# Layer 3's cross attention begun inside layer 2's read-back of expert rows, with stack rows 3 partitions apart

## The reference

```python
x = x + L2_xattn(layernorm(x), ctx, ...)     # 16 heads of 16 features
x = x + L2_ffn(layernorm(x), ...)            # 8 experts, 2 chosen per token, one shared expert
x = x + L3_xattn(layernorm(x), ctx, ...)
x = x + L3_ffn(layernorm(x), ...)

Q, K, V = heads(h @ Wq), heads(ctx @ Wk), heads(ctx @ Wv)
scores = einsum('bhnd,bhmd->bhnm', Q, K) * SCALE
out = softmax(scores) @ V                    # per head, then heads side by side
return out @ Wo + bo
```

## Time and profile before

| | us |
|---|---|
| median of 3 runs | 2535.56 (2533.76 to 2538.5) |
| the profiled execution's own time | 2525.97 |
| its span, first to last instruction | 2524.3 |
| TensorE busy | 2225.2 (88%) |
| VectorE busy | 1240.3 (49%) |
| ScalarE busy | 1044.0 (41%) |
| GpSimd busy | 535.8 (21%) |

### The profile page before, as it was taken

The page is one execution under the profiler, slowest core; times in us unless marked ns, Lnnn a source line. Parts: engine busy times, 40 slices in busy tenths (PEclk is TensorE's granted clock), DMA queues, the critical chain, the costliest instruction groups (busy, mean ns, idle before and its releaser), DMA issues. The chain is left out here.

```text
span 2524.3 us, 42831 instructions
## 1 busy us (share of the span) xinstructions
PE 2225.2 (88%) x13610; PEld 1643.9 (65%) x13611; DVE 1240.3 (49%) x2762; ACT 1044.0 (41%) x2555; POOL 535.8 (21%) x556
## 2 busy tenths in 40 slices
PE   8998399569998999898898998999997499989998
PEld 5664298444565874466785664679997256568887
DVE  4664300369876329876434664100000456577764
ACT  1564133214565523466532663124443036654332
POOL 1000200310122430121551000220001410054443
PEclk9999699789999999999998999999999699999999
DMA  7771143110000000000008741123221386110001
GB/s 190 154 173 70 46 169 109 46 42 0 26 0 15 26 17 0 25 0 3 13 6 143 133 79 74 36 106 121 73 106 47 99 154 129 36 34 20 26 25 34
DMA packets 110836, 164.29 MB, mean 65 GB/s; under 512 B 15273, under 2 KB 95257, under 8 KB 105721
## 3 DMA queue, kind: packets, MB, share of 16 engines
q1 hardware_dynamic: 101712, 140.68, 22.1%
q0 software_dynamic: 7680, 20.98, 2.6%
q10 hardware_dynamic: 1320, 1.03, 0.2%
HBM read 114.96 MB, written 47.32 MB: 64 GB/s over the span
## 5 line engine op out<-in xcount | busy, mean ns | idle before, releaser
L1043 DVE TENSOR_REDUCE xa_mx<-ps 128x2 f32<-128x512 f32 x384 | 247.0, 686 | 100.6 <-PE ps L695 99.5
L141 PE MATMUL ps<-ones 128*128 128x384 f32 (+1 forms) x450 | 164.7, 495 | 98.6 <-DMA ex_rows<-rows_out,rows_back 37.7
L902 ACT ACTIVATE xn_tok<-ps 128x512 f32<-128x512 f32 x384 | 210.6, 602 | 52.6 <-PE ps L703 50.4
L1482 PEld LDWEIGHTS ps<-ex_xT,ex_w 128*128 128x128 f32 x1792 | 210.5, 193 | 7.2 <-issue 4.4
L1482 PE MATMUL ps<-ex_xT,ex_w 128*128 128x128 f32 x1792 | 211.1, 276 | 3.8 <-issue 3.8
L1489 PE MATMUL ps<-ex_w,ex_h 128*128 128x256 f32 x896 | 202.7, 379 | 0.0
L141 PEld LDWEIGHTS ps<-ones 128*128 128x128 f32 x450 | 91.0, 223 | 142.9 <-issue 49.9
L695 PE MATMUL ps<-xa_ks,xa_qs 48*128 48x256 f32 (+1 forms) x768 | 157.7, 323 | 27.7 <-DMA xa_qs<-x_queries 9.1
L2147 PE MATMUL ps<-lo_w,lp_hs 128*128 128x512 f32 x384 | 176.1, 610 | 4.5 <-ACT lp_hs L2194 2.8
L1489 PEld LDWEIGHTS ps<-ex_w,ex_h 128*128 128x128 f32 x896 | 165.9, 190 | 20.2
L695 PEld LDWEIGHTS ps<-xa_ks,xa_qs 48*128 48x128 f32 (+1 forms) x768 | 106.6, 192 | 102.0 <-DVE xa_mx L1043 52.2
(11 more groups left out here) (343 smaller groups left out, 4815.8 us busy)
## 6 DMA issues: line engine op xcount, KB each, us to landing
xa_ks<-x_keys SPq DMA_DIRECT2D x144, 128.0 KB
xa_qs<-x_queries SPq DMA_DIRECT2D x144, 128.0 KB, 4.6
ex_w<-in_L0f_w_dram SPq DMA_DIRECT2D x16, 1024.0 KB, 7.0
ex_w<-in_L2f_w_dram SPq DMA_DIRECT2D x16, 1024.0 KB, 6.8
x_keys<-xa_khl SPq DMA_DIRECT2D x24, 512.0 KB, 5.6
x_queries<-xa_qhl SPq DMA_DIRECT2D x24, 512.0 KB, 3.0
ex_stage<-rows_in POOLq DMA_DIRECT2D x64, 128.0 KB, 2.3
rows_out<-ex_rows SPq DMA_DIRECT2D x56, 128.0 KB, 1.7
```

The source lines that it names most:

```text
L141: self.nc.tensor.matmul(self.ps[:, bank, 0:wide * P], self.ones[:], self.ones[:].unsqueeze(1).to_broadcast([P, wide, P]), start=True, stop ...
L902: nc.scalar.activation(pT[:, h % SLOTS].rearrange("p k q -> p (k q)"), c.ps[:, S_BANK + (HEADS * b + n) % 3], ACT.Exp).then_inc(exped.sem, 1)
L1043: nc.vector.tensor_reduce(mx[:, half, :, col], c.ps[:, M_BANK + h % 2].rearrange("p (t n) -> p t n", t=2), AX_X, ALU.max).then_inc(max_put ...
L1482: ins = nc.tensor.matmul(c.ps[:, f % 4, 0:P], w1[:, buf, k, f * P:(f + 1) * P], xT[:, k], start=(k == 0), stop=(k == KD - 1))
```

## The change

First, the parts of `xattn_phase` that were functions inside its engine blocks are now functions of the phase, which take the engine as an argument. With `room` given, `xattn_phase` is a generator that hands these functions out before it opens its own phase, and `expert_phases` calls them in its read-back. This is done for layer 2's experts with layer 3's attention:

```diff
+def experts_with_attention(c):
+    with ExitStack() as ctx:
+        room = c.sb("room", [P, tile_count(2), D], ctx=ctx)[:]
+        attention = xattn_phase(c, "L3x_", biased=True, room=room)
+        expert_phases(c, "L2f_", room, next(attention))
+        run(attention)
...
 (SyncE, behind the zeros)
+            if ahead:
+                sp.wait_ge(*out_stored(16 * tiles))
+                nxt.fetch_weights(sp)
+                for b in range(3):
+                    nxt.send_keys(sp, b)
+                    nxt.stack_keys(sp, b)
+                for b in range(2):
+                    nxt.send_queries(sp, b)
+                    nxt.stack_queries(sp, b)
...
 (TensorE)
-            pe.wait_ge(*back[2](16 * top * QUART))
+            if ahead:
+                pe.wait_ge(*nxt.weights_in(16))
+                for b in range(3):
+                    nxt.project_keys(pe, b)
+                    c.keep_busy(2, 0)
+                for b in range(2):
+                    nxt.turn_rows(pe, b)
+                    c.keep_busy(2, 0)
+                    pe.wait_ge(*nxt.scaled(1))
+                    nxt.project_queries(pe, b)
+                    c.keep_busy(2, 0)
+            pe.wait_ge(*back[2 + ahead](16 * top * QUART))
             c.keep_busy(8, 0)
...
 (ScalarE)
+            if ahead:
+                nxt.set_rows(act)
+                for b in range(3):
+                    nxt.lead_keys(act, b)
+                for b in range(2):
+                    nxt.put_rows(act, b)
+                    nxt.lead_queries(act, b)
...
 (VectorE, ahead of the additions, and in their loop)
+            if ahead:
+                nxt.scale_queries(dve)
+                for b in range(3):
+                    nxt.rest_keys(dve, b)
...
-                tile_stats(c, t)
+                ins = tile_stats(c, t)
+                if ahead and t == 3:
+                    nxt.find_moments(dve, 0, ins)
+                    for b in range(2):
+                        nxt.normalise_rows(dve, b)
+                elif ahead and t % 4 == 3 and t < 12:
+                    nxt.rest_queries(dve, t // 8)
...
 (GpSimd, in the loop of the gathers)
+            if ahead:
+                nxt.set_consts()
             for t in range(NT):
...
+                if ahead and t == 7:
+                    nxt.find_rstd(pool, 0)
```

Third, the form of the stacks, in all three attentions. The columns of Wq, Wk and the biases are reordered on their way in (`by_row`), so that in DRAM a row holds one feature of a head, and under it the eight pairs follow each other:

```diff
-                parts = dram["x_keys"][b].rearrange("(a g j r) t -> a j r g t", a=2, g=PAIRS, j=2)
+            parts = dram["x_keys"][b].rearrange("(a j r g) t -> a j r g t", a=2, g=PAIRS, j=2)
                 for j in range(2):
                     for n, part in enumerate((0, 0, 1)):
-                        at = 64 * j + HD * n
-                        sp.dma_start(ks[at:at + HD, b % K_BUFS].bitcast(F32), parts[part, j]
+                    at = 64 * j + n
+                    sp.dma_start(ks[at:at + 3 * HD - 2:3, b % K_BUFS].bitcast(F32), parts[part, j]
```

More of the change, by code:

```diff
@@ L493, in xattn_phase @@
     K_LOADS = 6 + 2 * masked
+    ahead = room is not None
     with ctx:
@@ new lines, in turn_rows @@
+        def turn_rows(pe, b):
+            if masked and b == 0:
+                pe.wait_ge(*ident_in(16))
+            pe.wait_ge(*normed(b + 1))
+            if ahead and b < 2:
+                pe.wait_ge(*k_rest(3))
+                pe.wait_ge(*q_rest(b))
+            elif b < 3:
+                pe.wait_ge(*k_rest(b + 1))
+                pe.wait_ge(*v_put(b - 1))
+            else:
+                pe.wait_ge(*v_put(b - 1))
+            for k in range(KD):
+                for t in range(2):
+                    ins = nc.tensor.transpose(c.ps[:, W_BANK, k * S + t * P:k * S + (t + 1) * P],
+                                              xs[:, 2 * (b % 2) + t, k * P:(k + 1) * P], c.ident[:])
+            ins.then_inc(turned.sem, 1)
@@ new lines, in project_keys @@
+        def project_keys(pe, b):
+            if ahead and b < 3:
+                pe.wait_ge(*k_rest(b))
+            else:
+                pe.wait_ge(*q_rest(b))
+            if b == 2 and not ahead:
+                pe.wait_ge(*v_put(1))
+                if masked:
+                    pe.wait_ge(*ctx_in[1](16))
+            for ch in range(KD):
+                for k in range(KD):
+                    ins = nc.tensor.matmul(c.ps[:, W_BANK, ch * S:(ch + 1) * S], wk[:, k, ch * P:(ch + 1) * P],
+                                           c.ctxT[:, k, b * S:(b + 1) * S], start=(k == 0), stop=(k == KD - 1))
+            ins.then_inc(k_proj.sem, 1)
@@ new lines, in project_queries, with put_rows @@
+        def project_queries(pe, b):
+            pe.wait_ge(*x_put(b + 1))
+            for ch in range(KD):
+                for k in range(KD):
+                    ins = nc.tensor.matmul(c.ps[:, W_BANK, ch * S:(ch + 1) * S], wq[:, k, ch * P:(ch + 1) * P],
+                                           c.xT[:, k, b * S:(b + 1) * S], start=(k == 0), stop=(k == KD - 1))
+            ins.then_inc(q_proj.sem, 1)
+        def put_rows(act, b):
+            act.wait_ge(*turned(b + 1))
+            nc.scalar.copy(c.xT[:, :, b * S:(b + 1) * S], bank).then_inc(x_put.sem, 1)
@@ new lines, in find_moments @@
+        def find_moments(dve, n, measured=None):
+            lo, hi = GROUPS[n]
+            if masked:
+                dve.wait_ge(*x_in[n](16))
+                for t in range(lo, hi):
+                    measured = tile_stats(c, t)
+            if measured:
+                chain.link(dve, measured)
+            st, at = c.stats[:, lo:hi], (slice(None), slice(lo, hi))
+            chain.link(dve, moments.join(dve, chain, at, (st[:, :, 0, 1], st[:, :, 1, 1]),
+                                         (st[:, :, 0, 2], st[:, :, 1, 2]), D // 4, mean[at], moments.total[at]))
+            nc.vector.tensor_scalar(var[at], moments.total[at], 1.0 / D, EPS, ALU.mult, ALU.add
+                                    ).then_inc(variance.sem, 1)
+            count[0] = chain.n
@@ L571, in _ @@
+        @block.sync
+        def _(sp):
+            if not ahead:
+                fetch_weights(sp)
             if masked:
@@ L1080, in _ @@
                 if h == 11:
[L1081 to L1083 removed]
+                    normalise_rows(dve, 2)
+                elif h == 13 and not ahead:
+                    rest_keys(dve, 2)
             for b in range(B):
```

540 lines of the change are left out of this document (269 added, 271 removed).

## The result

The changed kernel takes 2498.84 us in the median of 4 runs (2496.46 to 2507.45); the kernel before, beside it, 2534.66 us. The ratio is 0.987, with a 95% interval of 0.9851 to 0.989: 33 us faster, 28 to 38.

| us | before | after | gain | predicted |
|---|---|---|---|---|
| layer 0: to its last addition | 229.60 | 225.05 | 4.6 | 8.9 |
| layer 2: start to last addition | 213.58 | 207.21 | 6.4 | 7.4 |
| store of zeros to layer 3's last addition | 262.89 | 243.25 | 19.6 | 22.9 |

A forecast was written before the change was run, and what follows sets the result against it. TensorE was taken to bound layer 3's batch loop and GpSimd's gather chain the read-back. Layer 3 -22.9, layer 0 -8.9 and layer 2 -7.4 sum to -39.2 us, from 2535.56 to 2496 us; range 2484 to 2517.

The forecast's parts named there:

- The signs of the order: Read-back and layer 3: listed orderings that would show the forecast right, with the ninth tile's gather 6 to 9 us after the eighth's.
- Size of the hold: Layer 2's read-back: GpSimd's power waits for the variance with gathers queued behind it, moving the second half by +7.2 us.
- some 4 us: Read-back: time key copy 2 waits for the send of batch 1's keys, issued at about 1963.3 behind six stack DMAs.
- the rival's 4.5 us: Read-back: if stacks are no faster, the second send waits behind one, third rest 4.5 us later; 2517 us, chance 0.13.
- First stage of layer 3: From layer 3's phase start to its batch loop: about 15 us, with the turn of the maxima at about 8.7 us.
- The split of the first memsets' semaphore changes nothing there: Layers 0 and 2: no gain from the split, since TensorE's fillers end later than the normalising.
- Rate of the stacks: Stack transfers: between 134 and 269 GB/s, taken near the upper; 169 needed to remove the lead-in waits of layers 0 and 2.
- the DMA share with stacks falls under 1: Sign of a right forecast: the DMA engines' busy share while stacks fill the queues, 1.12 before, drops below 1.
- a long row is worse than eight short ones: Stack transfers: a long single row per queue makes each DMA slower, deciding from 1.34 us per DMA; chance 0.04.
- Layer 0: Layer 0's attention: -2.4 us wait for stacks, -3 clock, -3.5 waits for maxima; -8.9 us together.
- Layer 2: Layer 2's attention: -3.9 us wait for stacks, -2.5 clock, -1 waits for maxima; -7.4 us together.
- slower than before: Rival: at 1.6 us per stack DMA every one of the 24 batches waits, 2604 us; chance 0.04.

The follow-up runs named there:

- t3: Changed kernel with the second batch's keys sent before the first batch's stacks are issued, in layer 2's read-back; ratio to the kernel before 0.9848.
- t1: Changed kernel with additions of tiles 0 to 3 and their moments ahead of the third key rest, plus 24 one-element ScalarE copies; ratio to before 0.9844.
- s1_move_only: Changed kernel with the stacks as before (1 KB pieces, 16 partitions side by side), lead-in still moved under the read-back; ratio to before 0.9934.
- r3: Changed kernel; in layer 3 alone VectorE finds the moments of the last 12 tiles behind its fourth maximum; ratio to before 0.9862.
- t4: Changed kernel with second keys sent ahead of first stacks, fillers behind the third quarter, moments behind the fourth maximum; 2490.91 us, ratio to before 0.9829.
- s3: Kernel before with stack rows in 8 KB pieces, still on 16 partitions side by side; nothing moved; ratio to before 1.0041.
- s4: Kernel before with stack rows 3 partitions apart, still in 1 KB pieces; nothing moved; ratio to before 0.9921.
- r2: Changed kernel with TensorE's eight fillers in the read-back waiting for the third quarter of the gathers instead of the last; ratio to before 0.9863.
- t2: Changed kernel with the fillers behind the third quarter of the gathers and layer 3's moments of 12 tiles behind the fourth maximum; ratio to before 0.9849.

## Why the prediction was right, and where it was not

Forecast 2496 us in a range of 2484 to 2517; measured 2498.84. The mechanism and the order of size were right; that the medians lie only 3 us apart is luck. The profiled execution was to take 2487 us and took 2496.46: by the traces the gain is 29.5 us, not 39.2. Against that, the prediction carried over the 9.6 us by which the profiled execution of before lay under its median; in the changed kernel this difference is 2.4 us. The two errors nearly cancel. Point by point:

- **What bounds the kernel, and the chain of the hold: right.** The signs of the order all came: first addition behind the third rest, power behind the variance, fillers last, first score at once, no score that waits for stacked keys (three buffers), none for wo. t3 and t1 moved the chain's links one by one, and the gathers followed (4.4 and 7.5 us). One sign missed its size: the ninth tile's gather starts 10.1 us after the last one of the eighth, not 6 to 9.
- **Size of the hold: +7.2 predicted, 10.0 measured.** The steps that were too small are "some 4 us" for the landing of the second send, 6.0 measured, and the stack's issue ahead of it, 3.69 instead of 2.68 us. The 5.2 us behind a stack was the row with the same neighbour. The longer issue was not to blame by itself: with the old stacks (`s1_move_only`) it was 2.71 us, but the send behind it took 7.3, and the third rest ended at +26.1, not sooner than at +25.8. So the rival's 4.5 us for slow stacks ahead of the second send did not come either. The phase started 12.2 us later instead of 9.8.
- **First stage of layer 3: 15 us predicted, 17.8 measured.** The miss lies ahead of the turn of the maxima, which came 12.7 us into the phase instead of 8.7; from there to the loop it was 5.1 us instead of 6.3. The first maximum stood at 2.7 us instead of 1.9, because VectorE, released after the first memset, ran its moments into GpSimd's second one (0.9 in r3, where they are out of its way). And TensorE's clock was 0.50 from 2004.69 to 2009.69, where the value projection took 3.46 us (1.99 in t4). The stage's length goes with this clock, which the sum did not price: 14.7 us in t4, where it was 1.00 from 5 us into the phase on, 20.1 in t3, where it was 0.50, 0.84 and 0.50. "The split of the first memsets' semaphore changes nothing there" was said of layers 0 and 2, and holds: 229.37 and 213.74 us in `s1_move_only`. On the other side the batch loop of layer 3 gave 1.9 us that the sum left out (162.6 to 160.7 us; with the old stacks, in `s1_move_only`, 163.1).
- **Rate of the stacks: right effect, wrong reason and size.** I took a rate near 269 GB/s, "since an 8 KB row resembles a plain tile's row". Measured 160 (164 in the trace after), below the 169 needed, and the piece size had no clear part in the gain: s3 is slower than before, s4 has it all by its ratio. The row with 269 GB/s was also of another kind of traffic: before the stack issued at 2031.11 it had mainly two sends out of SBUF, the other way round (384 and 377 GB/s in its first two microseconds, 88 and 227 in the others). The rule that I set beside it, the Trainium skill's "SBUF — State Buffer", section "Door 1: The DMA port swizzle" (the write rate follows the number of ports that the partitions reach), points at what made the difference, and spacing alone agrees with it in direction; its 104 GB/s for four ports and 196 for eight lie further apart than the 124 to 131 and 150 to 160 seen here. One spacing was tried, so that the ports are the reason is not shown by these runs alone. The sign "the DMA share with stacks falls under 1" did not come: it fell from 1.12 to 1.02. The rival "a long row is worse than eight short ones" had no mechanism in the profile; packed, it came true by 10 us.
- **Layer 0: 8.9 predicted, 4.6 measured.** Its terms came: the first wait fell from 2.38 to 0.99 us, the clock from 38 to 46 rose from 0.71 to 1.00, and scores wait 2.3 us for maxima instead of 5.4. But a wait took their place. The fourteen stack DMAs of batch 1 (two are of the mask) are issued one behind the other in 8.7 us instead of 7.1, from the same time on (45.5 and 45.7), since the first waits for a send. TensorE is done with its lead-in at 53.5 instead of 58.5, waits 4.33 us for these stacks, and starts its loop at 57.84 instead of 59.22; behind it the clock is lower, as a row of before and one of after show:

```profile
54.00:62.00 8.00, 6.41 (x37) 3.73 (x36) 5.51 (x9) 3.11 (x7) 0.00 (x0) 0.93 0.70 138
```

```profile
57.84 0.55 PE L819 MATMUL ps<-xa_ks,xa_qs 49*128 49x256 f32 x1 [4.33 <-DMA xa_qs<-x_queries]
...
54.00:62.00 8.00, 4.16 (x21) 3.23 (x22) 2.58 (x4) 2.63 (x6) 0.00 (x0) 0.50 0.69 160
```

- **Layer 2: 7.4 predicted, 6.4 measured.** The wait went from 3.90 to 1.66 us, not to nothing, and the clock behind it still fell, to 0.66 in 1345 to 1353. The signs "no score waits for queries in layers 0 and 2" (0.99, 4.33 and 1.66 us in the trace after) and "the clock stays near 1" did not come.
- **The rival "slower than before"**: far off for the changed kernel, no score waited for stacked keys.

## What to carry over

Where many small-row transfers fill the queues, ask first on which partitions they land, not how long their pieces are: the same bytes, three partitions apart, moved at 150 GB/s instead of 124, and small transfers on a critical path stopped waiting; then count the dearer issue, which becomes the next wait. When work is moved under a chain, list in each engine's order what now stands ahead of the chain's own instructions: here one key rest ahead of four additions held 16 gathers, and one send issued ahead of six stack DMAs gave 4.4 us of that back. A wait that is removed is worth its length only up to the next transfer: in layer 0 TensorE came to its loop 5 us sooner and waited 4.3 of them there, with the clock down behind it. And where the same stage takes 14.7 or 20 us with the clock, one profiled execution does not tell what an edit of a few us is worth.

## What was not expected of the hardware

- In layer 3's loop a stack DMA onto spaced rows costs its issuer 0.61 us with 8 KB pieces and 0.63 with 1 KB, one onto packed rows 0.44 and 0.45.
- Two VectorE operations on 128x12 elements took 1.34 and 1.26 us instead of 0.17 and ended when GpSimd's memset beside them did, while the three operations on two tensors ahead of them, under the same memset, took 0.17 to 0.18. The Trainium skill's "SBUF — State Buffer", section "Who interferes with whom", says just this: an operation on two tensors does not contend with a GpSimd instruction that only writes, a tensor-scalar one can take a mode that needs the shared ports and then waits for the whole instruction. The trace agrees for the first (a tensor-scalar one, begun 0.5 us after the memset); the second reads two tensors and stands behind it in VectorE's order.
- ScalarE was idle 16.3 and 17.5 us in two kernels on one chip with no semaphore that ended it, while gathers ran without a pause. The same chip took 22 us more from the last addition of layer 2's attention to the store of zeros (431.7 us in r2, 409.2 in t2), which is as much as the kernel before is slower there (2555.83 and 2533.09 us).
